# A decoder layer with routed experts: up and down weight parts fetched and awaited apart, gate and product ahead of the up splits

## The reference

```
x = layernorm(x + attention(x))                      # 16 heads
x = layernorm(x + quantised_gated_mlp(x, fside, ctx))
x = layernorm(x + moe(x))

# moe: 16 routed experts of inner width 352, two shared ones
cw  = weights of the best 4 of 16 experts per token (0 for the others)
h   = silu(x @ w1[e]) * (x @ w3[e])
y   = sum over e of cw[:, e] * (h @ w2[e])
z   = silu(x @ sw1) * (x @ sw3) @ sw2
moe = y + z
```

## Time and profile before

| what | value |
|---|---|
| median of three runs | 1454.87 us |
| the profiled execution | 1448.41 us |
| its span, first to last instruction | 1446.4 us |
| mean granted clock of TensorE | 0.962 |
| PE busy | 1314.7 us, 91% |
| DVE busy | 867.7 us, 60% |
| ACT busy | 439.0 us, 30% |
| routed tiles: first `up` at 873.60 us, last at 1407.73 us | 534.1 us |

### The profile page before, as it was taken

One profiled execution on the slowest core, in us unless ns is written; L12 is line 12 of the kernel. 1 busy time (PEld: TensorE's weight loads), 2 busy tenths in 40 slices (PEclk: granted clock), 3 DMA queues, 4 the chain that ended last, 5 costly groups with the idle time before them and its releaser, 6 DMA issues.

```text
span 1446.4 us, 24161 instructions
## 1 busy us (share of the span) xinstructions
PE 1314.7 (91%) x7375; PEld 984.3 (68%) x7375; DVE 867.7 (60%) x1455; ACT 439.0 (30%) x651; POOL 402.7 (28%) x495
## 2 busy tenths in 40 slices
PE   7998899989898999889999998999999999879991
PEld 3554445445544555478978887999999988768891
DVE  2443877587758776887668875334433445465534
ACT  1132243414441254232211013223322334353423
POOL 1131013200240015000103832344433444333432
PEclk9999999999999999999999999999999999989996
DMA  8441533233521533504110005445454466768447
GB/s 291 127 100 38 166 86 101 75 119 87 147 75 44 131 103 88 175 20 149 67 36 30 30 29 176 85 79 140 96 119 85 96 149 155 190 183 238 75 75 256
DMA packets 89593, 163.14 MB, mean 113 GB/s; under 512 B 8528, under 2 KB 29520, under 8 KB 89440
## 3 DMA queue, kind: packets, MB, share of 16 engines
q1 hardware_dynamic: 72640, 121.83, 27.2%
q0 software_dynamic: 16816, 39.59, 14.7%
HBM read 112.37 MB, written 49.02 MB: 112 GB/s over the span
## 4 chain that ended last, share of the span: by engine, by line
PE 71%; DVE 14%; DMA 5%; issue 5%; ACT 3%; SPq 1%; DVEq 1%; POOL 1%; ACTq 0%; POOLq 0%
PE psR L1140 14%; PE psUA L1040 12%; PE psUB L1040 11%; PE psY L1047 8%; PE psR L1047 5%; PE psOT L1261 4%; PE psR L1230 3%; PE psST L1244 3%; PE psTX L1023 2%; PE psTH L1056 2%; DMA room<-in_L_ffn_w_dram 2%; PE psR L1154 2%; DVE nm L1639 2%; DVE w_s L1317 1%; DVE xs L1555 1%
## 5 line engine op out<-in xcount | busy, mean ns | idle before, releaser
L1040 PE MATMUL psUA<-w_s,xgT 128*128 (+1 forms) x1284 | 243.1, 340 | 8.1 <-DVE xgT L1437 4.0
L1040 PE MATMUL psUB<-w_s,xgT 128*128 (+1 forms) x1284 | 225.5, 325 | 0.0
L1040 PEld LDWEIGHTS psUA<-w_s,xgT 128*128 128x128 f32 x1284 | 213.8, 196 | 14.4 <-issue 5.5
L1040 PEld LDWEIGHTS psUB<-w_s,xgT 128*128 128x128 f32 x1284 | 211.4, 190 | 0.0
L852 POOL DMA_INDIRECT sx_d<-yg,dst_i x74 | 119.4, 1614 | 302.7 <-ACT yg L930 269.6
L892 ACT ACTIVATE silg<-psUA 128x352 f32<-128x352 f32 x107 | 49.5, 462 | 402.3 <-PE psUB L1040 402.3
L1047 PE MATMUL psY<-w_s,hgT 128*128 (+3 forms) x621 | 160.8, 403 | 0.2 <-issue 0.2
L1446 DVE SCALAR_TENSOR_TENSOR hg<-silg,cws,psUB 128x352 f32<-128x352 f32 x75 | 43.5, 580 | 175.3 <-ACT silg L892 175.3
L814 POOL TENSOR_SCALAR_AFFINE_SELECT pT<-pT 128x128 f32<-128x128 f32 (+1 forms) x192 | 61.3, 336 | 297.2 <-ACT pT L970 297.0
L1639 DVE TENSOR_REDUCE nm<-psR 128x1 f32<-128x128 f32 (+3 forms) x256 | 111.8, 486 | 38.9 <-PE psR L1232 35.9
L1047 PEld LDWEIGHTS psY<-w_s,hgT 128*128 128x128 f32 (+1 forms) x621 | 112.6, 189 | 22.0 <-issue 0.4
(11 more groups left out here) (229 smaller groups left out, 1911.6 us busy)
## 6 DMA issues: line engine op xcount, KB each, us to landing
room<-in_L_ffn_w_dram SPq DMA_DIRECT2D x32, 704.0 KB, 5.9
scr_d<-qhl SPq DMA_DIRECT2D x32, 512.0 KB, 3.8
qst<-scr_d SPq DMA_DIRECT2D x48, 256.0 KB, 4.1
kst<-scr_d SPq DMA_DIRECT2D x48, 256.0 KB, 6.1
room<-in_L_ffn_w_dram SPq DMA_DIRECT2D x16, 512.0 KB, 7.5
xt<-in_x_dram SPq DMA_DIRECT2D x4, 1024.0 KB, 7.7
xr<-in_x_dram SPq DMA_DIRECT2D x4, 1024.0 KB, 5.2
breg<-in_fside_BxS2xS_dram SPq DMA_DIRECT2D x4, 1024.0 KB, 8.5
```

Source lines behind the costliest of these rows:

```text
L1040: mm = pe.matmul(t[:, 0:F], xgT[:, par, a_, c * P:(c + 1) * P], w[:, buf, b_, c, :], start=(c == 0 and n == 0), stop=(c == C - 1 and n == ...
```

## The change

The semaphore of the weights' transfers becomes two, one for w1 and w3 (s_wup), one for w2 (s_wdown), and SP fetches the up part of an expert as soon as the up part of the raw slot is split, before it waits for the down split. ACT waits for the part that it splits. And in `one` of ACT and of DVE, the gate and the gated product stand ahead of the UP splits. The number of instructions of each engine stays as it was, but for waits.

```diff
-        s_w = sem("s_w")
+        s_wup = sem("s_wup")
+        s_wdown = sem("s_wdown")
...
                 sp.wait_ge(s_wlo, 2 * (e + 1))
                 apart(sp)
+                sp.wait_ge(s_wup, 32 * (e + SH))
+                apart(sp)
+                weights(sp, s_wup, [(w1_r[:, par], w1_v[:, bass.ds(e, 1)]), (w3_r[:, par], w3_v[:, bass.ds(e, 1)])])
                 sp.wait_ge(s_w2lo, e + 1)
                 apart(sp)
-                sp.wait_ge(s_w, 64 * (e + SH))
+                sp.wait_ge(s_wdown, 32 * (e + SH))
                 apart(sp)
-                weights(sp, [(w1_r[:, par], w1_v[:, bass.ds(e, 1)]), (w3_r[:, par], w3_v[:, bass.ds(e, 1)]),
-                             (w2_r[:, par, 0:NKF - 1, :], w2[bass.ds(e, 1), 0:W2K, :].rearrange("e (k p) d -> p (e k) d", p=P)),
+                weights(sp, s_wdown, [(w2_r[:, par, 0:NKF - 1, :], w2[bass.ds(e, 1), 0:W2K, :].rearrange("e (k p) d -> p (e k) d", p=P)),
                              (w2_r[0:F - W2K, par, NKF - 1, :], w2[bass.ds(e, 1), W2K:F, :].rearrange("e p d -> p (e d)"))])
...
         def _(act):
             def split(e, buf, which):
 
-                act.wait_ge(s_w, e * 64 + 64)
-                apart(act)
+                for landed in [s_wup] * (UP[0] in which or UP[1] in which) + [s_wdown] * (DOWN[0] in which):
+                    act.wait_ge(landed, e * 32 + 32)
+                    apart(act)
...
             def one(j, par, facts):
+                gate(j + NH)
                 if_first(act, facts, split, UP)
-                gate(j + NH)
                 if not is_last(j, RT):
                     high_x(j + (NT + 1), 1 - par)
...
             def one(j, par, facts):
+                weighted(j)
                 if_first(dve, facts, split, UP)
-                weighted(j)
                 if not is_last(j, RT):
                     low_x(j + (NT + 1), 1 - par)
```

More of the change, by code:

```diff
@@ L388, in decoder_layer, with weights @@
         W2K = (len(KF) - 1) * P
-        def weights(sp, parts_):
+        def weights(sp, landed, parts_):
             for dst, src_ in parts_:
-                sp.dma_start(dst, src_).then_inc(s_w, 16)
+                sp.dma_start(dst, src_).then_inc(landed, 16)
         stA.close()
@@ L628, in shared_expert @@
                 rows = sw2[s * F:(s + 1) * F, :]
-                weights(sp, [(w1_r[:, s], sw1_v[:, s]), (w3_r[:, s], sw3_v[:, s]),
-                             (w2_r[:, s, 0:NKF - 1, :], rows[0:W2K, :].rearrange("(k p) d -> p k d", p=P)),
+                weights(sp, s_wup, [(w1_r[:, s], sw1_v[:, s]), (w3_r[:, s], sw3_v[:, s])])
+                weights(sp, s_wdown, [(w2_r[:, s, 0:NKF - 1, :], rows[0:W2K, :].rearrange("(k p) d -> p k d", p=P)),
                              (w2_r[0:F - W2K, s, NKF - 1, :], rows[W2K:F, :])])
@@ L715, in walk @@
                     elif x == ("split", 0):
-                        sp.wait_ge(s_w, 64)
+                        sp.wait_ge(s_wup, 32)
+                        sp.wait_ge(s_wdown, 32)
                         shared_expert(1)
```

## The result

The changed kernel takes 1508.69 us (median of four runs, 1506.6 to 1510.85); the kernel before takes 1455.05 in the runs beside it. That is 53.6 us slower by the medians. The ratio over all runs is 1.035, with a 95% interval of 1.0321 to 1.0378, or 50.9 us. The forecast was 1491 with a range of 1468 to 1508, so the sign and the mechanism came as forecast.

What follows compares the result with a forecast made beforehand. PE, busy 91% of the span, was taken to bound the kernel. First tiles 22.2, tile 0 1.4 and clock 17 summed to 40.6 us slower, giving 1489 or 1495.5; 1491 was taken, range 1468 to 1508.

Steps and rivals of the forecast that it cites:

- The path: In first tiles, UP splits start behind the gate, low_x behind the splits, and PE's next `up` waits for low_x.
- the rival of the freed PE: Next `up` doesn't wait for the splits: first tiles take 6.95 us, 27.5 us less, 1421 to 1427; chance 0.05.
- The stall, 10.5 us a first tile at full clock: First tiles of experts 1 to 14 take 10.5 us against 6.95 with weights landed; PE idles 3.5 us.
- the term of 22.2 us: 14 first tiles at 10.5 us, 147.0, against 124.8 before including two tiles' excess behind them: 22.2 us slower.
- Tile 0, 1.4 us: The first routed tile goes from 9.15 to 10.5 us by the same chain: 1.4 us slower.
- The transfers: Expert weight fetches: no wait for weights counted any more; earlier fetching gives nothing beyond what slower tiles give anyway.
- The clock, 17 us: PE's clock falls behind 12 of 14 first tiles' idle times, 1.4 us each: 17 us slower, bounds 0 and 19.6.
- the longer kind as a rival: Clock falls for longer, 2.33 us behind all 14 first tiles: 56 us slower, 1505 to 1511; chance 0.12.
- Small edits: Branch around UP splits in 60 other tiles, two semaphores, later evacuate and scatter: 0, upper end 7 us.
- The base: Starting time for the added loss: 1448.4 us profiled gives 1489, the median, 6.5 us higher, gives 1495.5; 1491 taken.
- The three terms: Routed first tiles 22.2, tile 0 1.4 and lower clock 17 us: 40.6 us slower in all.
- a third term of 0: No lower clock behind PE's stalls in first tiles: 23.6 us slower, 1472 to 1478; as a rival, chance 0.17.

Runs made afterwards that it cites:

- experiment 3: Changed kernel with the next rows' high and low parts also ahead of the UP splits on ACT and DVE: 1468.35 us, ratio 1.0075.
- Experiment 5: Changed kernel with 28 useless matmuls on PE behind `turned` in first tiles: 1491.42 us; control with one such matmul: 1516.82 us.
- experiment 6: Nothing changed: the kernel before and the changed kernel each profiled once more, 1449.96 and 1510.34 us.
- experiment 2: The kernel before with the new order alone, one semaphore and the four transfers together: 1506.72 us, ratio 1.032.

## Why the prediction was right, and where it fell short

- **The path.** Right. PE is released by low_x, not by hg (54.9 of its 60.4 us ahead of psUA), and the rival of the freed PE is out: 40 us come back when the next rows are put ahead of the splits (experiment 3).
- **The stall, 10.5 us a first tile at full clock.** Right to 0.02 us (10.52), and with it the term of 22.2 us.
- **Tile 0, 1.4 us.** It took 10.91 us against 9.15: 1.8.
- **The transfers.** Right that the new order hides them: with and without the separate fetches it takes 1508.7 and 1506.7. ACT's 20.7 us of waiting for them fell to 2.0.
- **The clock, 17 us.** This is the term that was mis-sized. It took 12 falls at 1.4 us. The clock fell behind all 14, and the falls cost 25.6 us, 1.83 each: 160.36 - 147.0 = 13.4 in first tiles that start in the lower clock, and 12.2 in the seven tiles behind that are no first tiles. The price of a fall was too low more than the count was. The 1.4 us came from the two tiles behind falls of the earlier trace rows, and the changed kernel shows nine such ones (1.3 to 1.5 us over, as the 8.27), but also five longer ones (2.2 to 2.7 over, as the 9.48). Experiment 5 measured nearly the same by itself: 25.4 us by the medians, 22.6 of it in those 21 tiles of the two profiles. I had the longer kind as a rival (2.33 a tile in all 14) and held it to follow longer idle times only. That was wrong: behind the same 3.5 us come both. The measured 1508.69 lies in that rival's span too (1505 to 1511), but its price for all 14 isn't borne out.
- **Small edits.** 0, as assumed.
- **The base.** The three terms gave 1495.5 us on the median and 1489 on the profiled execution, and I took 1491. On the median, which is what was measured, the forecast gives away 4.5 us by that choice alone.

The sum by steps is 22.2 + 1.8 + 25.6 = 49.6, and the routed stage grew by 49.9 and 48.7 us in two pairs of profiles. The median grew by 53.6, and the ratio's interval, 46.7 to 55.0, holds that sum. Some 4 us of the 53.6 are in no step; the time ahead of tile 0 varies by more than that (experiment 6), but no run shows that they come from there.

The page of the Trainium skill (TensorE: Matmul & The Clock Gate, section Why this matters for your kernels) that speaks against idle gaps between bursts was borne out in each of the 14, though not in all such cases of the other kernels (13 of 14 in experiment 2). What the same page says of the VectorE copy (section Loop structure matters more than you think) it says of a loop in which the next matmuls follow at once. It doesn't reach an idle time of 3.5 us that a VectorE chain ends, and I shouldn't have drawn a third term of 0 from it.

## What to carry to other kernels

When a wait on one path is moved out of the way, follow the other inputs of the same consumer: here the product was ready 5 us ahead of the next rows, and PE needs both. Work that runs in a window in which its engine has nothing else to do is nearly free there (0.2 us a first tile for the splits before). Elsewhere it costs what stands behind it and is waited for: 3.6 us a first tile in the changed kernel, 0.7 in experiment 3. So a reorder is judged by that window, and by what its new place stands ahead of. And an edit with two halves is worth taking apart: one half (the fetches) was a gain of 0.7 to 0.8% that the other hid.

## What was not expected of the hardware

- The same idle time of TensorE, 3.5 us, was followed by spells of the lower clock of two lengths: in the changed kernel they cost 1.3 to 1.5 us in nine cases and 2.2 to 2.7 in five. Of the seven first tiles there that start at full clock, the four with a granted clock of 0.97 to 1.00 had the shorter kind behind them, and the three with 0.92 or 0.93, in which the clock fell earlier, the longer. The order-only kernel has an exception to this (0.97, then 2.8 us), and in it one idle time of 3.5 us was followed by full clock. Behind idle times of 2.3 us the clock fell in 10 of 14 cases. Filling the idle time with 28 small matmuls kept it at full in all 14.
- A sequencer's read of one table value from on-chip memory, 0.30 us at the median, took 0.6 to 1.0 us in up to 10 of some 150 cases, mostly while expert weights landed. The landing isn't needed for it: a third read behind the other two took 0.88 us at the median, in ordinary tiles too (experiment 5). What makes a read long stays open. That one can hold up TensorE is seen twice, with two reads in a row (7.82 us, idle for 0.86) and with a read by itself (7.99 us, idle for 0.83).
